# Keys of two chunks placed by tables of slots, a table load of its own, and the positive part moved to VectorE

## The chip, the cores and the metric

The kernel runs on one core of one Trainium2 chip. The metric is the device time in microseconds (us), from the start to the end of one execution. In the rows, PE is TensorE (PEld its weight loads), DVE is VectorE, ACT is ScalarE, POOL is GpSimd and SP is the queue that issues most transfers.

## What is computed

Two layers over 2 x 2048 tokens of width 128, in fp32. Layer 0 is a long convolution through Fourier transforms and a mixture of 8 experts computed densely, with a shared one. Layer 1 is linear attention and a mixture of 8 experts of which each token takes two. The change touches the keys of layer 1's attention and what stands beside them:

```python
def _fm(t):
    return jax.nn.elu(t) + 1.0
q = _fm((x @ wq + bq).reshape(B, N, H, Dh))
k = _fm((x @ wk + bk).reshape(B, N, H, Dh))
v = (x @ wv + bv).reshape(B, N, H, Dh)
kv = jnp.einsum('bnhd,bnhe->bhde', k, v)
z = 1.0 / (jnp.einsum('bnhd,bhd->bnh', q, k.sum(axis=1)) + 1e-06)
scores = jnp.einsum('bnhd,bhde,bnh->bnhe', q, kv, z)
...
topk_scores, topk_idx = jax.lax.top_k(scores, K)
g = jnp.einsum('ner,efr->nef', gate_hidden, W_B)
up = jnp.einsum('nh,efh->nef', x, W_up)
y = jnp.einsum('nef,ehf->neh', jax.nn.silu(g) * up, W_down)
```

Here elu(t) + 1 is computed as max(t, 0) + exp(-max(-t, 0)).

## The kernel before

The tokens are 32 tiles of 128, and 4 tiles are a chunk; there are 8 chunks, numbered 0 to 7. Each engine runs one list of instructions in order, and waits on semaphores. The second half of the program is written as slots: on every engine a loop runs over 90 slots, and in each slot it emits a few steps in a fixed order. Slots 0 to 47 hold layer 0's experts, six slots to a chunk. In each, TensorE multiplies a gate and an up projection (`gate0`, `up0_step`) and, one slot later, the down projection (`down0_step`); ScalarE takes silu of the gate (line 1159) and VectorE multiplies (`product0`, line 1597). `gate0` of a slot stands first on TensorE, then the keys, then `up0_step`. `up0_step` waits until the product of the slot before has read its bank.

Slots 52 to 87 hold layer 1's 36 pairs of blocks of sorted rows: rows are transposed and split in a high and a low part (`turn_rows`, `rows_hi` line 1086, `rows_lo` line 1610), multiplied (`gate_up`), go through silu (line 1093) and a product (`product`, line 1618), which frees the bank that the next pair's `gate_up` needs, and then through the down projection (`turn_products`, `down_rows`). Slots 48 to 51 hold neither: they are the tail of layer 0's last chunks and the head of layer 1.

The work of layer 1's norm, router and attention for chunk c is spread over the slots behind it. `due(s, at)` gives the chunk whose step stands in slot s = 6 (c + 1) + at:

```python
def due(s, at):
    c, rest = divmod(s - at, N0)
    return c - 1 if rest == 0 and 0 <= c - 1 < NCH else None
```

For the keys of chunk c, which are two halves j = 2c and 2c + 1 of two tiles, the steps were: `keys_values` on TensorE, a tile at each of 7, 8, 10, 11; `key_bias` on VectorE at 9 and 12 (line 1580, out of one PSUM bank); `key_features` on ScalarE at 13, for both halves (lines 1076, 1078, 1079: the negative part, the positive part, the exponential) and `query_exp` (line 1133); `key_sum` and `query_features` on VectorE at 14 (lines 1668, 1675); `key_value_sum` on TensorE at 15 and 16. The third tile's `keys_values` waits for the first half's `key_bias`, since both halves use one bank:

```python
if h == 0 and j:
    pe.wait_ge(kv_bias, j)
```

Other steps that are named below: `residual` and its statistics on VectorE at 1 (line 1411), `negated_mean` at 3 (line 1419), `normalise1` on ScalarE at 3 (line 1058), `normed_lo` at 6 (line 1588), the router's gates on TensorE at 7 to 10, their squares on ScalarE at 8 to 11 (line 1067) and sums on VectorE at 9 to 12 (`norm_sum`, line 1462); `rank` (lines 1220 to 1228, 1474) and `tables` (lines 1524 to 1570) on VectorE for every second chunk. silu and exp stand in different tables of ScalarE's functions, and the compiler puts an ACT_TABLE_LOAD where the next function needs the other one.

## Time and profile before

| | us |
|---|---|
| median of 3 runs | 627.75 (625.75 to 628.34) |
| the profiled execution | 624.3 |
| its span | 622.3 |
| busy: PE / DVE / ACT / POOL | 559.3 / 433.8 / 314.8 / 297.3 |

The span is the time from the first to the last instruction of the core; 2.0 us lie around it. The busy times of the engines overlap. Slot 19, where chunk 0's keys are turned to features, starts at 320 us of the span; layer 0's last product is at 430.8 and pair 0's silu at 444.9. Rows of a timeline give the start, the duration, and in brackets the idle time of the engine before the row with what ended it. Consecutive instructions of an engine overlap a little, so the distance from one start to the next is the cost in the stream.

### The profile page before, as it was taken

Reading aid. Unit: us, or ns where it says so; the run is one execution under the profiler, and the core shown is the slowest. Engines: PE = TensorE matmul, PEld = TensorE weight load, DVE = VectorE, ACT = ScalarE, POOL = GpSimd, SP = SyncE. Lnnn points to the kernel's source line nnn. Section 1 sums busy time; section 2 is a strip of 40 time slices with the busy share of each in tenths; the row PEclk is TensorE's granted clock in tenths of the full one; section 3 lists DMA queues with packets and bytes.
Section 4 is the critical chain, followed back from the end, with each engine's and each line's share of the span. In section 5 each row is a group of like instructions: output and inputs, shape, how many; then the busy total and the mean of one; then the engine's idle time right before and its main releaser. Section 6 shows DMA issues by size and latency. Waiting matters only on the chain.

```text
span 622.3 us, 10595 instructions
## 1 busy us (share of the span) xinstructions
PE 559.3 (90%) x3218; PEld 467.3 (75%) x3218; DVE 433.8 (70%) x1151; ACT 314.8 (51%) x623; POOL 297.3 (48%) x268
## 2 busy tenths in 40 slices
PE   5899999999989898999999999998789887899970
PEld 2879986586778676788888888877568777788870
DVE  5958998908941596434565898998878894466673
ACT  4470336764523444144465774675675843365550
POOL 4630030004561355147333446877636775477770
PEclk9999999999999999999999999999999898899995
DMA  7341030410030520323222223303212232233626
GB/s 212 144 203 70 2 135 9 93 43 1 1 136 0 182 111 1 93 71 94 86 81 79 63 73 98 92 27 117 67 53 67 69 107 74 65 86 88 226 85 228
DMA packets 48381, 54.94 MB, mean 88 GB/s; under 512 B 7029, under 2 KB 40374, under 8 KB 47271
## 3 DMA queue, kind: packets, MB, share of 16 engines
q1 hardware_dynamic: 43542, 42.99, 22.1%
q0 software_dynamic: 4320, 8.99, 4.2%
q10 hardware_dynamic: 466, 2.31, 1.7%
q8 instruction: 28, 0.46, 0.3%
q14 instruction: 25, 0.20, 0.1%
HBM read 36.22 MB, written 15.94 MB: 84 GB/s over the span
## 4 chain that ended last, share of the span: by engine, by line
PE 31%; DVE 10%; issue 8%; POOL 7%; ACT 6%; DMA 3%; SPq 0%; POOLq 0%; ACTq 0%; DVEq 0%
PE banks L1759 4%; PE banks L1761 4%; PE banks L1760 4%; PE banks L2116 3%; PE banks L1965 3%; PE banks L1879 2%; DMA arena<-result_rows 2%; POOL arena L887 2%; PE banks L1871 2%; PE banks L2101 2%; POOL result_rows L872 1%; DMA result_rows<-arena 1%; POOL expert_rows L857 1%; PE banks L1892 1%; PE banks L1893 1%
## 5 line engine op out<-in xcount | busy, mean ns | idle before, releaser
L872 POOL DMA_INDIRECT result_rows<-arena x71 | 69.0, 972 | 31.8 <-issue 17.2
L821 POOL TENSOR_TENSOR arena<-arena 128x512 f32<-128x512 f32 x32 | 40.7, 1273 | 86.2 <-DVE arena L1443 86.2
L857 POOL DMA_INDIRECT expert_rows<-arena x64 | 63.2, 988 | 30.9 <-issue 15.8
L887 POOL TENSOR_TENSOR arena<-arena 128x512 f32<-128x512 f32 x32 | 42.4, 1324 | 64.9 <-DVE arena L1597 64.8
L1597 DVE TENSOR_TENSOR arena<-banks,arena 128x512 f32<-128x512 f32 x48 | 33.0, 688 | 42.4 <-PE banks L1761 33.4
L1965 PEld LDWEIGHTS banks<-arena 128*128 128x128 f32 x384 | 48.8, 191 | 7.5 <-POOL arena L887 3.6
L1965 PE MATMUL banks<-arena 128*128 128x128 f32 x384 | 51.6, 277 | 2.5 <-POOL arena L887 1.5
L1871 PE MATMUL banks<-arena 128*128 128x512 f32 x96 | 50.5, 608 | 2.4 <-DVE arena L1443 1.1
L1879 PEld LDWEIGHTS banks<-arena 128*128 128x128 f32 x256 | 33.0, 191 | 19.0 <-POOL arena L821 14.4
L1159 ACT ACTIVATE arena<-banks 128x512 f32<-128x512 f32 x48 | 28.7, 599 | 36.2 <-PE banks L1761 31.7
L2116 PE MATMUL banks<-arena 128*128 x284 | 40.6, 289 | 6.3 <-ACT arena L1110 5.9
L979 ACT ACTIVATE arena<-banks 128x512 f32<-128x512 f32 x48 | 28.7, 597 | 32.5 <-PE banks L1847 32.5
L2116 PEld LDWEIGHTS banks<-arena 128*128 128x128 f32 x284 | 36.8, 202 | 7.4 <-issue 7.4
L1008 ACT ACTIVATE arena<-banks 128x512 f32<-128x512 f32 x32 | 19.1, 597 | 39.5 <-PE banks L1879 39.5
L1441 DVE TENSOR_TENSOR arena<-banks,arena 128x512 f32<-128x512 f32 x32 | 22.1, 692 | 23.7 <-PE banks L1871 22.1
L1879 PE MATMUL banks<-arena 128*128 128x128 f32 x256 | 34.4, 277 | 4.0 <-POOL arena L821 4.0
L1759 PE MATMUL banks<-projection_hi,xnt_hi 128*128 128x384 f32 (+1 forms) x92 | 33.0, 359 | 2.6 <-DVE xnt_lo L1259 2.6
L1759 PE MATMUL banks<-gate_up_weights_hi,rows_hi 128*128 x71 | 32.0, 450 | 3.5 <-DVE arena L1618 3.5
L1450 DVE TENSOR_TENSOR arena<-banks,arena 128x512 f32<-128x512 f32 x16 | 11.1, 692 | 34.5 <-PE banks L1893 34.5
L1618 DVE TENSOR_TENSOR arena<-banks,arena 128x512 f32<-128x512 f32 (+1 forms) x36 | 24.5, 680 | 15.0 <-ACT arena L1093 14.7
L1093 ACT ACTIVATE arena<-banks 128x512 f32<-128x512 f32 (+1 forms) x36 | 21.4, 594 | 24.0 <-PE banks L1761 23.9
L1110 ACT ACTIVATE arena<-banks,arena 128x128 f32<-128x128 f32 x71 | 22.2, 364 | 21.7 <-DMA result_rows<-arena 11.5
(277 smaller groups left out, 1625.7 us busy)
## 6 DMA issues: line engine op xcount, KB each, us to landing
arena<-expert_weights SPq DMA_DIRECT2D x64, 128.0 KB, 3.4
arena<-expert_rows SPq DMA_DIRECT2D x71, 66.0 KB, 1.9
arena<-in_x SPq DMA_DIRECT2D x8, 512.0 KB, 7.0
arena<-result_rows SPq DMA_DIRECT2D x8, 512.0 KB, 5.7
arena<-in_dft_f SPq DMA_DIRECT2D x1, 2048.0 KB, 9.5
normed_hi<-xnt_hi SPq DMA_DIRECT2D x1, 2048.0 KB, 6.7
normed_lo<-xnt_lo SPq DMA_DIRECT2D x1, 2048.0 KB, 11.1
arena<-in_dft_i SPq DMA_DIRECT2D x1, 2048.0 KB, 7.6
```

The source lines that it names most:

```text
L821: nc.gpsimd.tensor_tensor(out=T1[:, q % 3, :], in0=T1[:, q % 3, :], in1=T2[:, q % 2, :], op=ALU.add).then_inc(y_in, 1)
L857: pool.indirect_dma_start(out=xrows, out_offset=bass.IndirectOffsetOnAxis(ap=SLOT[:, k, t:t + 1], axis=0), in_=XNF[:, t, :], in_offset=Non ...
L872: pool.indirect_dma_start(out=yrows, out_offset=bass.IndirectOffsetOnAxis(ap=DEST[:, i, n:n + 1], axis=0), in_=YB[:, i % YBUFS, n, :], in_ ...
L887: nc.gpsimd.tensor_tensor(out=AM0[slot % 2], in0=AM0[slot % 2], in1=WB0[:, m, :], op=ALU.mult).then_inc(weighted, 1)
L979: nc.scalar.activation(spread_rows(n % NI), bank(spread_bank(n % NI), 2, NGR, 4), ACT.Copy)\
L1159: nc.scalar.activation(SG0, PS[0], ACT.Silu).then_inc(silu_done, 1)
L1597: nc.vector.tensor_tensor(out=AM0[n % 2], in0=PS[1], in1=SG0, op=ALU.mult).then_inc(mult_done, 1)
L1759: mm(o, lh, rh, start=start, stop=False, skip_group_check=True)
L1871: mm(PS[2 + J % 2], TURNF, ZT[:, J % 2, :], start=True, stop=True).then_inc(d_mm, 1)
L1879: ins = mm(PS[6 + q % 2][:, P * n:P * (n + 1)], T1[:, q % 3, P * n:P * (n + 1)], TURNI, start=True, stop=True)
L1965: ins = mm(PS[2][:, D * t:D * (t + 1)], AM0[n % 2][:, P * t:P * (t + 1)], DW0[:, m, :], start=False, stop=(m == N0 - 1), skip_group_check= ...
L2116: ins = mm(PS[6][:, P * s:P * (s + 1)], AMT[:, i % 2, 2 * s + f, :], DN_FLAT[:, at], start=(f == 0), stop=(f == 1), skip_group_check=True)
```

## The change

Tables of slots, one entry for each chunk, take the place of the fixed numbers. Chunks 0 to 4 keep theirs. Chunk 5's third and fourth tile come one slot earlier, and so does everything behind them (features in slot 48, sums in 49, `key_value_sum` in 50). Chunk 6's keys come in slots 49 and 50, its biases in 50 and 51, its features in 51 (they were in 55), its sums in 52, its products in 53 and 54. Chunk 7's first negative part comes at 10 and not at 13. On ScalarE the negative parts of both halves now stand ahead of both exponentials; the positive part (line 1078) is gone, and VectorE's sum takes it in one scalar_tensor_tensor. Behind chunk 6's exponentials a silu of one column is added, whose result nobody reads.

```diff
+KEYS_AT = (*((7, 8, 10, 11),) * 5, (7, 8, 9, 10), (7, 7, 8, 8), (7, 8, 10, 11))
+KEY_BIAS_AT = (*((9, 12),) * 5, (9, 11), (8, 9), (9, 12))
+KEY_NEG_AT = (*((13, 13),) * 5, (12, 12), (9, 9), (10, 13))
+KEY_EXP_AT = (*(13,) * 5, 12, 9, 13)
+KEY_SUMMED_AT = (*(14,) * 5, 13, 10, 14)
+KEY_VALUE_AT = (*((15, 16),) * 5, (14, 14), (11, 12), (15, 16))
...
+        def chunks_due(s, table):
+
+            return [c for c in range(NCH) if s == N0 * (c + 1) + table[c]]
+
+        def parts_due(s, table):
+
+            return [(c, n) for c in range(NCH) for n, at in enumerate(table[c]) if s == N0 * (c + 1) + at]
...
-            def key_features(j):
+            def key_negative(j):
...
                 nc.scalar.activation(KEX[:, j % 3], k, ACT.Relu, scale=-1.0).then_inc(k_neg, 1)
+            def key_exp(j):
+
                 act.wait_ge(k_neg, j + 1)
-                nc.scalar.activation(k, k, ACT.Relu)
                 nc.scalar.activation(KEX[:, j % 3], KEX[:, j % 3], ACT.Exp, scale=-1.0).then_inc(k_exp, 1)
...
-                c = due(slot, 13)
-                if c is not None:
-                    key_features(2 * c)
-                    key_features(2 * c + 1)
+                for c, h in parts_due(slot, KEY_NEG_AT):
+                    key_negative(2 * c + h)
+                for c in chunks_due(slot, KEY_EXP_AT):
+                    key_exp(2 * c)
+                    key_exp(2 * c + 1)
                     query_exp(c)
+                    if c == NCH - 2:
+                        act.wait_ge(k_sum, 2 * c)
+                        nc.scalar.activation(KEX[:, (2 * c - 1) % 3, 0, 0:1], BQ, ACT.Silu)
...
-                nc.vector.tensor_tensor(out=k, in0=k, in1=KEX[:, j % 3], op=ALU.add).then_inc(k_sum, 1)
+                nc.vector.scalar_tensor_tensor(out=k, in0=k, scalar=0.0, in1=KEX[:, j % 3], op0=ALU.max,
+                                               op1=ALU.add).then_inc(k_sum, 1)
...
+                for c, t in parts_due(slot, KEYS_AT):
+                    keys_values(TPC * c + t)
```

The changed file's lines are 14 to 20 further down. What the tables do to the lists of instructions, at three places:

TensorE in slot 45, before. The first three rows are `gate0`, the next three `up0_step`, L2052 is `key_value_sum`.

```order
L1759 MATMUL banks<-normed_chunk_hi,gate_weights_hi 128x512 [waits silu_done]
L1760 MATMUL banks<-normed_chunk_lo,gate_weights_hi 128x512
L1761 MATMUL banks<-normed_chunk_hi,gate_weights_lo 128x512
L1759 MATMUL banks<-normed_chunk_hi,up_weights_hi 128x512 [waits mult_done]
L1760 MATMUL banks<-normed_chunk_lo,up_weights_hi 128x512
L1761 MATMUL banks<-normed_chunk_hi,up_weights_lo 128x512
L2052 MATMUL banks<-arena 128x129 [waits kv_mask,k_sum]
```

The same place of the changed kernel:

```order
L1777 MATMUL banks<-normed_chunk_hi,gate_weights_hi 128x512 [waits silu_done]
L1778 MATMUL banks<-normed_chunk_lo,gate_weights_hi 128x512
L1779 MATMUL banks<-normed_chunk_hi,gate_weights_lo 128x512
L1777 MATMUL banks<-qkv_weights_hi,normed_hi 128x256 [waits kv_bias]
L1778 MATMUL banks<-qkv_weights_lo,normed_hi 128x256
L1779 MATMUL banks<-qkv_weights_hi,normed_lo 128x256
L1777 MATMUL banks<-normed_chunk_hi,up_weights_hi 128x512 [waits mult_done]
```

The keys of chunk 5's third tile, with their wait for the first half's bias, now stand ahead of slot 45's up projection.

VectorE in slots 49 to 51, before, from the end of `residual`: L1220 to L1228 are `rank` of the third router batch, L1668 and L1675 the sums of chunk 5, L1580 the first `key_bias` of chunk 6.

```order
L1206 TENSOR_SCALAR arena<-arena 128x4 [waits dve_chain]
L1220 TENSOR_TENSOR arena<-arena 128x512 [waits log1_in]
L1221 TENSOR_TENSOR arena<-arena 128x512 [waits dve_chain]
L1668 TENSOR_TENSOR arena<-arena 128x2x128 [waits k_exp,dve_chain]
L1668 TENSOR_TENSOR arena<-arena 128x2x128 [waits k_exp]
L1675 TENSOR_TENSOR arena<-arena 128x512 [waits q_pos,q_exp]
L1227 TENSOR_TENSOR arena<-arena 128x512
L1228 TENSOR_TENSOR arena<-arena 128x512 [waits dve_chain]
L1610 TENSOR_TENSOR rows_lo<-banks,rows_hi 128x256 [waits xt_hi,dve_chain]
L1580 TENSOR_TENSOR arena<-banks,arena 128x2x256 [waits kvs_mm,kv_mm]
L1419 SCALAR_TENSOR_TENSOR arena<-arena 128x4 [waits ln1_rstd]
```

And changed:

```order
L1226 TENSOR_SCALAR arena<-arena 128x4 [waits dve_chain]
L1688 SCALAR_TENSOR_TENSOR arena<-arena 128x2x128 [waits k_exp] x2
L1696 TENSOR_TENSOR arena<-arena 128x512 [waits q_pos,q_exp]
L1240 TENSOR_TENSOR arena<-arena 128x512 [waits log1_in]
L1241 TENSOR_TENSOR arena<-arena 128x512 [waits dve_chain]
L1600 TENSOR_TENSOR arena<-banks,arena 128x2x256 [waits kvs_mm,kv_mm,dve_chain]
L1247 TENSOR_TENSOR arena<-arena 128x512
L1248 TENSOR_TENSOR arena<-arena 128x512 [waits dve_chain]
L1630 TENSOR_TENSOR rows_lo<-banks,rows_hi 128x256 [waits xt_hi,dve_chain]
L1600 TENSOR_TENSOR arena<-banks,arena 128x2x256 [waits kvs_mm,kv_mm]
L1439 SCALAR_TENSOR_TENSOR arena<-arena 128x4 [waits ln1_rstd]
```

Chunk 6's first bias stands between the two halves of `rank`, and its second ahead of `negated_mean`; chunk 5's second bias, further up, is gone from slot 48.

ScalarE in slots 51 and 52, before: `rows_hi`, a square, `normalise1` of chunk 7 in two rows, `rows_hi` of pair 1, a square, and pair 0's silu with its table load.

```order
L1086 ACTIVATE rows_hi<-banks 128x256 [waits xt_mm]
L1067 ACTIVATE arena<-banks 128x512 [waits log1_in,gh_mm]
L1058 ACTIVATE arena<-arena 128x128 [waits ln1_nmr]
L1058 ACTIVATE arena<-arena 128x128 x3
L1086 ACTIVATE rows_hi<-banks 128x256 [waits xt_mm]
L1067 ACTIVATE arena<-banks 128x512 [waits log1_in,gh_mm]
L1093 ACT_TABLE_LOAD
L1093 ACTIVATE arena<-banks 128x512 [waits gu_mm]
```

And changed:

```order
L1072 ACTIVATE arena<-arena 128x128 [waits ln1_nmr]
L1072 ACTIVATE arena<-arena 128x128 x3
L1090 ACTIVATE arena<-arena 128x256 [waits kvs_mm,kv_bias] x2
L1095 ACTIVATE arena<-arena 128x256 [waits k_neg] x2
L1149 ACTIVATE arena<-arena 128x512 [waits q_neg]
L1196 ACT_TABLE_LOAD
L1196 ACTIVATE arena<-arena 128x1 [waits k_sum]
L1102 ACTIVATE rows_hi<-banks 128x256 [waits xt_mm]
L1081 ACTIVATE arena<-banks 128x512 [waits log1_in,gh_mm]
L1109 ACTIVATE arena<-banks 128x512 [waits gu_mm]
```

Five activations, the load and the one-column silu now stand ahead of pair 1's `rows_hi`. Slots 55 and 56 have lost an exp load and a silu load: the changed program has 18 table loads in all, and the one before 20.

## Rows read from the trace of the kernel before

**Rows 1.** The page: busy time and share of each engine.

```profile
PE 559.3 (90%) x3218; PEld 467.3 (75%) x3218; DVE 433.8 (70%) x1151; ACT 314.8 (51%) x623; POOL 297.3 (48%) x268
```

**Rows 2.** Windows: length, busy PE, PEld, DVE, ACT, POOL, granted clock, DMA share, GB/s.

```profile
320.40:409.30 88.90, 88.26 (x551) 76.75 (x550) 75.33 (x191) 58.05 (x110) 51.85 (x42) 1.00 0.26 76
```

**Rows 3.** Timeline of ScalarE in slot 19: chunk 0's features.

```profile
320.94 0.41 ACT L1076 ACTIVATE arena<-arena 128x256 f32<-128x256 f32 x1
321.38 0.42 ACT L1078 ACTIVATE arena<-arena 128x256 f32<-128x256 f32 x1
...
324.49 0.62 ACT L1133 ACTIVATE arena<-arena 128x512 f32<-128x512 f32 x1
```

**Rows 4.** Timeline of VectorE, slots 45 to 47: chunk 5's first bias, then products.

```profile
422.65 0.69 DVE L1580 TENSOR_TENSOR arena<-banks,arena 128x512 f32<-128x512 f32 x1
...
423.32 0.69 DVE L1597 TENSOR_TENSOR arena<-banks,arena 128x512 f32<-128x512 f32 x1
...
430.77 0.69 DVE L1597 TENSOR_TENSOR arena<-banks,arena 128x512 f32<-128x512 f32 x1 [1.70 <-ACT arena L1159]
```

**Rows 5.** Timeline of TensorE: slot 45's up projection, and slot 46's keys.

```profile
419.61 0.50 PE L1759 MATMUL banks<-normed_chunk_hi,up_weights_hi 128*128 128x512 f32 x1 [0.58 <-DVE arena L1597]
...
423.39 0.39 PE L1759 MATMUL banks<-qkv_weights_hi,normed_hi 128*128 128x256 f32 x1
```

**Rows 6.** Timeline of VectorE, slots 49 to 51.

```profile
433.76 0.68 DVE L1411 TENSOR_TENSOR arena<-banks,arena 128x512 f32<-128x512 f32 x1
...
435.88 0.68 DVE L1220 TENSOR_TENSOR arena<-arena 128x512 f32<-128x512 f32 x1
...
437.33 0.77 DVE L1668 TENSOR_TENSOR arena<-arena 128x256 f32<-128x256 f32 x2
...
438.62 0.68 DVE L1227 TENSOR_TENSOR arena<-arena 128x512 f32<-128x512 f32 x1
...
440.06 0.42 DVE L1610 TENSOR_TENSOR rows_lo<-banks,rows_hi 128x256 fp32r<-128x256 f32 x1
440.40 0.68 DVE L1580 TENSOR_TENSOR arena<-banks,arena 128x512 f32<-128x512 f32 x1
```

**Rows 7.** Timeline of ScalarE, slots 51 and 52: the stretch ahead of pair 0's silu.

```profile
441.19 1.65 ACT L1058 ACTIVATE arena<-arena 128x128 f32<-128x128 f32 x4 [3.07 <-DVE arena L1419]
...
443.60 1.28 ACT L1093 ACT_TABLE_LOAD   x1
444.90 0.60 ACT L1093 ACTIVATE arena<-banks 128x512 f32<-128x512 f32 x1
```

**Rows 8.** Timeline of VectorE, slots 55 to 57: the end of `tables`, pairs 4 and 5.

```profile
459.42 0.81 DVE L1538 TENSOR_TENSOR arena<-arena 128x16 f32<-128x16 f32 x4
461.58 0.42 DVE L1610 TENSOR_TENSOR rows_lo<-banks,rows_hi 128x256 fp32r<-128x256 f32 x1 [1.36 <-ACT rows_hi L1086]
463.90 0.69 DVE L1618 TENSOR_TENSOR arena<-banks,arena 128x512 f32<-128x512 f32 x1 [1.90 <-ACT arena L1093]
```

**Rows 9.** Timeline of TensorE: four rows that follow an idle stretch.

```profile
440.63 0.41 PE L2072 MATMUL banks<-arena 128*128 128x128 f32 x2 [1.40 <-DVE rows_lo L1610]
...
489.62 1.09 PE L2101 MATMUL banks<-arena 128*128 128x128 f32 x4 [2.15 <-ACT arena L1100]
...
524.21 0.79 PE L2116 MATMUL banks<-arena 128*128 x2 [2.88 <-ACT arena L1110]
...
536.96 0.75 PE L2116 MATMUL banks<-arena 128*128 x3 [2.12 <-ACT arena L1110]
```

**Rows 10.** Windows behind the first two of these stretches, columns as in rows 2.

```profile
441.00:443.00 2.00, 1.92 (x9) 1.31 (x9) 1.93 (x8) 1.81 (x5) 1.52 (x2) 1.00 0.22 72
490.00:491.00 1.00, 1.00 (x7) 1.00 (x6) 0.55 (x2) 0.98 (x2) 0.79 (x1) 0.50 0.26 68
```

**Rows 11.** Groups by form on VectorE: count, busy us, mean ns, idle before.

```profile
L1668 DVE TENSOR_TENSOR arena<-arena 128x256 f32<-128x256 f32 x16 | 6.8, 463 | 0.8 <-ACT arena L1079 0.6
L1371 DVE SCALAR_TENSOR_TENSOR arena<-arena 64x1024 f32<-64x1024 f32 x2 | 2.4, 1207 | 0.0
```

More of the change, by code:

```diff
@@ L1690, in _ @@
                     residual(c)
-                for h in range(2):
-                    c = due(slot, 9 + 3 * h)
-                    if c is not None:
-                        key_bias(2 * c + h)
+                for c, h in parts_due(slot, KEY_BIAS_AT):
+                    key_bias(2 * c + h)
                 c = due(slot, 17)
@@ L1709, in _ @@
                     places_of(i)
-                c = due(slot, 14)
-                if c is not None:
+                for c in chunks_due(slot, KEY_SUMMED_AT):
                     key_sum(2 * c)
@@ L2176, in _ @@
                     turn_normed(c)
-                for h in range(2):
-                    c = due(slot, 15 + h)
-                    if c is not None:
-                        key_value_sum(2 * c + h)
+                for c, h in parts_due(slot, KEY_VALUE_AT):
+                    key_value_sum(2 * c + h)
                 c = query_due(slot, 0)
```

4 lines of the change are left out of this document (removed).

## The prediction

> **What bounds the kernel now.** I read the page first. TensorE is busy for 559.3 of 622.3 us, VectorE 434, ScalarE 315 [rows 1]. That is an average, so I took windows by stage. In layer 0's experts, 320.4 to 409.3 us, TensorE is busy 88.26 of 88.90 us [rows 2]: nothing that another engine saves there can show. The timelines then gave what each moved step does in its place: ScalarE's features [rows 3], the end of layer 0 on VectorE and TensorE [rows 4, 5], the head of layer 1 on VectorE and ScalarE [rows 6, 7], and the pairs behind it, where the three engines wait for each other in turn [rows 8]. From about 420 us on a delay on any of the three tends to reach the end, because a pair's product frees the bank of the next.
>
> **The positive part.** ScalarE loses two operations a chunk. One lies between 321.38 and the load, and the two together take 0.87 us: from 320.94 to 324.49 the features need 3.55 us, and 2.68 without them [rows 3]. For chunks 0 to 4 this is hidden under the full TensorE; I take -0.3 us, with 0 and 5 x 0.87 = -4.3 as bounds. VectorE's sum becomes a scalar_tensor_tensor. No such operation of 128x256 is in the trace. The additions take 463 ns in the mean, and a scalar_tensor_tensor of 1024 columns takes 1207 [rows 11]: (1207 - 463) / 768 = 0.97 ns a column, no more than an addition pays (0.69 us for 512, [rows 4]; 0.42 for 256, [rows 6]: 1.05 ns). So 0. Upper bound 0.25 us each, one more pass of 256 columns at that rate; 16 of them make 4 us. It may also be below the 463, which holds waiting for a shared port at most; that would give 16 x 0.04 = 0.6.
>
> The Trainium skill ("Vector Engine (DVE) Microarchitecture Reference", section 7, "Points that are easy to get wrong") says that a scalar_tensor_tensor with two sources in SBUF that aren't both bf16 runs at half the rate. By it each sum would take near 0.69 us, which is the upper bound just given. The 1207 ns of the 1024-column row don't agree with it; whether its operands are of that kind in every respect, no row shows.
>
> **Chunk 5's third tile (stall A).** It waits for chunk 5's first bias, and now stands ahead of slot 45's up projection. That bias runs at 422.65 on VectorE, behind `tables`, and is over at about 423.35 [rows 4]. TensorE has finished the gate at 419.0, and before the change started the up projection at 419.61, after 0.58 idle [rows 5]. Now it stands still until 423.35: 4.3 us of idle. The keys take 0.45, the up projection starts at 423.8 (+4.2). Its product ran at 423.32 [rows 4], since VectorE was held by `tables`: now 424.7 (+1.4). On TensorE the work of 419.61 to 423.39 stands behind; 0.36 comes back because slot 46's keys are gone from there, 0.6 of waits, and the product of slot 47 had 1.70 idle in front of it [rows 4]. It moves from 430.77 to 432.8 (+2.0). `residual` of chunk 7 moves by less, as chunk 5's second bias (0.69) is gone from before it: 433.76 [rows 6] to 435.2 (+1.4).
>
> **Chunk 6's keys (stall B).** Its third and fourth tile now stand in slot 50 and wait for its first bias. On VectorE that bias stands behind `residual` with its statistics (433.76 to 435.88, 2.1 us), the sums of chunk 5 (437.33 to 438.62, 1.3) and the first half of `rank` (435.88 to 437.33, 1.4) [rows 6]: 435.2 + 2.1 + 1.3 + 1.4 = 440.0, done at 440.7. In that time TensorE has done its router product and the two first tiles and waits for about 4 us. Then come the two key tiles (0.8), chunk 5's `key_value_sum` (0.9), the router's gates (0.8), `turn_rows` (0.4), and on ScalarE `rows_hi` (0.4): the first `rows_lo` goes from 440.06 [rows 6] to 444.1, **+4.0**. `negated_mean` stands behind it and behind the second bias, and `normalise1` goes from 441.19 [rows 7] to 445.2.
>
> **Features and table load.** Ahead of pair 0's silu on ScalarE there now stand two negative parts, two exponentials and the query's: 0.45 + 0.4 + 0.3 + 0.3 + 0.5, 1.8 us less a little by the distances of [rows 3], plus 0.3 for the silu of one column and its wait. The load of 1.28 only moves: it stood just before that silu, at 443.60 [rows 7]. Pair 0's silu was bound by ScalarE's own list, `normalise1` included, so the whole 2.1 is paid: 444.90 to 451.0, **+6.1** in all. On VectorE chunk 6's sums and query features, 1.3 us, stand in slot 52 ahead of the router's `norm_sum`, whose result the next square on ScalarE waits for, and behind that square stands pair 1's silu: **+1.2**. Together +7.3.
>
> **What comes back.** In slots 55 and 56 chunk 6's features with both their loads are gone. VectorE stood idle 1.36 and 1.90 us there: it had finished `tables` at 459.42 + 0.81 = 460.23, and `product` ran only at 463.90 [rows 8]. With only `rows_lo` (0.34 in the stream) between, -3.3. The sums and query features behind it, -1.3. Chunk 6's second bias out of slot 54, -0.2. At chunk 7 the same exponentials and loads stay, but one negative and both positive parts are gone in front of ScalarE's copy for which TensorE waits 2.15 us at 489.62 [rows 9]: -1.2. With -0.3 from layer 0 this makes -6.3, and +7.3 - 6.3 = **+1.0 us** at full clock.
>
> **The clock.** TensorE stands idle before four rows of [rows 9]. After 1.40 us at 440.63 the granted clock stays 1.00, 2.4 GHz; after 2.15 at 489.62 it is 0.50, 1.2 GHz [rows 10]. The same was so after 2.88 and 2.12 us at 524.21 and 536.96 [rows 9]. The price is seen at 489.62: four transposes take 1.09 us where the same count at full clock takes 0.60 or so, and the work up to the next full-clock row some 3.4 us in place of 1.8, **1.6 us**. Stalls A and B are both over 4 us, in places where TensorE does everything that follows: 2 x 1.6 = +3.2. No row has a fall directly behind layer 0's dense stage, so 0 to 3.3 each are the bounds (the longest low stretch, after 524.21, is twice as long). Sum: +1.0 + 3.2 = **+4.2 us**, 624.3 to 628.5 for the profiled execution; the median shown is 3.45 above it, so 627.75 + 4.2 = **632.0**.
>
> **Rivals.** A change by less than about 0.5% (3.1 us) can't be told from none in a measurement of this kernel.
> - *Stalls and clock falls*, the forecast: +4.2, own range +2.5 to +7 (630.2 to 634.7). Chance 0.46. For it: the order of the rows and the wait leave TensorE no choice in slot 45.
> - *Stalls at full clock, or partly taken up*: A's +1.4 at `residual` vanishes if VectorE has slack there, and no clock is lost: +1.0 down to -0.4, so 627 to 630. Chance 0.27. Against it: three falls in three idle stretches over 2 us. For it: the stalls are behind long dense work, and those three are not.
> - *Faster*, the other side: the wait in slot 50 doesn't bind, because VectorE comes to chunk 6's first bias before TensorE needs its bank. It is then free of the +4.0, and pays only 2.1 + 1.2 against 6.3: -3.0, and with part of the 4.3 hidden in layer 0 coming through, -3 to -5: 623 to 625. It decides at about 436 us for that bias; my sum has 440.0, and would have to count `rank` and the sums (2.7) and A (1.4) wrongly. Chance 0.20.
> - *The sum at half rate*: 16 x 0.25 = 4 us on VectorE, of which some 3 in places where it is waited for (the last chunks and their neighbours): 635. Chance 0.05; this is the rule named above.
> - *The silu of one column saves nothing because the load stays where it was*: the compiler's list already shows it at the new place, so this rival has 0.02, at +4.2 as well.
>
> **How the numbers follow.** The likeliest case gives 632.0. Slower by over 0.5% (above 630.9): most of the first case, 0.40, nearly all of the rate case and the last, 0.07: 0.47. Faster (below 624.6): 0.18 of the third and 0.04 of gains in layer 0 beside the second: 0.22. The rest, 0.31, lies between. The range of 623.5 to 634.5 leaves out the far end of the faster case, the half-rate case and a long low clock.
>
> **What the changed profile would show.** A: TensorE idle for about 4.3 us before keys (line 1777), released by VectorE's line 1600, and the up projection behind it near 423.8. B: a second such idle, some 4 us, before keys 3 and 4 of chunk 6, and the first `rows_lo` (line 1630) near 444. Granted clock 0.50 behind each. Line 1688 at about 0.42 to 0.46 us; 0.69 would be the half rate. One ACT_TABLE_LOAD with line 1196, none in slots 55 and 56, and pairs there at the 4 us of their neighbours. Chunk 7: a shorter idle before line 2119. I am wrong if the first stall is short, if the clock stays at 1.00 behind them, or if pair 0's silu isn't near 451.

## The result, and the profile after

The changed kernel takes 634.62 us in the median of 4 runs (630.37 to 637.33), and the kernel before 626.75 in the median of 4 (623.67 to 628.34). The ratio is 1.0159 with a 95% interval of 1.0111 to 1.0208: slower, +7.9 us by the medians. Forecast was +4.2 us, with a range up to 634.5. The direction, and the two stalls that were to make it, are right; the size is not. Below, "stall A" and "stall B" are the two of the prediction, a "fall" is a stretch in which TensorE's granted clock is 0.50 (1.2 GHz) and not 1.00 (2.4 GHz), and "low" means time in such stretches.

The page of the changed kernel, busy time and share (before: [rows 1]). ScalarE lost 8 us, TensorE's busy time grew by 10 with the same number of instructions:

```profile
PE 569.2 (90%) x3218; PEld 477.0 (75%) x3218; DVE 434.2 (68%) x1151; ACT 306.8 (48%) x606; POOL 297.6 (47%) x268
```

TensorE, timeline of slot 45 and of slots 50 to 53 (before: [rows 5, 9]):

```profile
424.92 0.40 PE L1779 MATMUL banks<-normed_chunk_hi,gate_weights_lo 128*128 128x512 f32 x1
429.66 0.38 PE L1777 MATMUL banks<-qkv_weights_hi,normed_hi 128*128 128x256 f32 x1 [4.34 <-DVE arena L1600]
...
448.45 0.58 PE L1777 MATMUL banks<-qkv_weights_hi,normed_hi 128*128 128x256 f32 x1 [3.67 <-DVE arena L1600]
...
449.89 1.92 PE L2070 MATMUL banks<-arena 128*128 128x129 f32 x8
...
454.48 0.79 PE L1777 MATMUL banks<-router_weights_hi,normed_hi 128*128 128x512 f32 x1 [0.96 <-ACT arena L1081]
...
460.91 0.59 PE L1777 MATMUL banks<-router_weights_hi,normed_hi 128*128 128x512 f32 x1 [1.92 <-ACT arena L1081]
```

Stall A is 4.34 us (forecast 4.3) and stall B 3.67 (forecast about 4), both before keys and both ended by the bias, line 1600. A third wait, 1.92 us before a router product at 460.91, wasn't forecast as one of TensorE.

VectorE in slots 45 and 49 to 51 (before: [rows 4, 6]):

```profile
428.92 0.69 DVE L1600 TENSOR_TENSOR arena<-banks,arena 128x512 f32<-128x512 f32 x1
...
442.87 0.68 DVE L1431 TENSOR_TENSOR arena<-banks,arena 128x512 f32<-128x512 f32 x1
...
444.98 0.76 DVE L1688 SCALAR_TENSOR_TENSOR arena<-arena 128x256 f32<-128x256 f32 x2
445.65 0.68 DVE L1696 TENSOR_TENSOR arena<-arena 128x512 f32<-128x512 f32 x1
446.25 0.69 DVE L1240 TENSOR_TENSOR arena<-arena 128x512 f32<-128x512 f32 x1
446.97 0.69 DVE L1241 TENSOR_TENSOR arena<-arena 128x512 f32<-128x512 f32 x1
447.70 0.69 DVE L1600 TENSOR_TENSOR arena<-banks,arena 128x512 f32<-128x512 f32 x1
...
454.05 0.42 DVE L1630 TENSOR_TENSOR rows_lo<-banks,rows_hi 128x256 fp32r<-128x256 f32 x1 [4.33 <-ACT rows_hi L1102]
```

Between `residual` and the bias that TensorE waits for stand the sums and half of `rank`, 444.98 to 447.70. Then VectorE itself waits 4.33 us for `rows_hi`, which waits for TensorE's late work.

ScalarE in slots 51 and 52 (before: [rows 7]):

```profile
455.17 1.65 ACT L1072 ACTIVATE arena<-arena 128x128 f32<-128x128 f32 x4 [0.74 <-DVE arena L1439]
456.73 0.71 ACT L1090 ACTIVATE arena<-arena 128x256 f32<-128x256 f32 x2
457.35 0.71 ACT L1095 ACTIVATE arena<-arena 128x256 f32<-128x256 f32 x2
457.96 0.62 ACT L1149 ACTIVATE arena<-arena 128x512 f32<-128x512 f32 x1
458.60 1.28 ACT L1196 ACT_TABLE_LOAD   x1
459.89 0.20 ACT L1196 ACTIVATE arena<-arena 128x1 f32<-128x1 f32 x1
460.00 0.37 ACT L1102 ACTIVATE rows_hi<-banks 128x256 fp32r<-128x256 f32 x1
460.26 0.59 ACT L1081 ACTIVATE arena<-banks 128x512 f32<-128x512 f32 x1
460.74 0.60 ACT L1109 ACTIVATE arena<-banks 128x512 f32<-128x512 f32 x1
```

The list runs without a gap from `normalise1` to pair 0's silu; the square at 460.26 is what TensorE's router product at 460.91 waited for.

Windows, columns as in [rows 2]: layer 0's experts, two windows behind stalls A and B, and the stage from 410 to 470 us:

```profile
327.20:415.60 88.40, 87.93 (x551) 76.66 (x550) 75.31 (x191) 55.17 (x102) 51.79 (x42) 1.00 0.27 76
431.50:433.50 2.00, 2.00 (x12) 2.00 (x11) 2.00 (x3) 0.00 (x0) 1.26 (x1) 0.50 0.00 0
449.00:456.00 7.00, 6.04 (x23) 4.84 (x22) 2.65 (x6) 1.70 (x5) 2.08 (x2) 0.50 0.08 20
410.00:470.00 60.00, 46.43 (x236) 38.10 (x234) 45.12 (x129) 30.46 (x62) 35.81 (x33) 0.86 0.18 56
```

The granted clock of 0.50 lasts from 447.5 to 457.8 us, 10 us: it begins inside stall B, which ends at 448.45. In [rows 10] it was about 3.4 us long behind one idle stretch.

The same window of the kernel before:

```profile
410.00:470.00 60.00, 49.30 (x284) 38.46 (x282) 50.00 (x163) 40.88 (x83) 38.59 (x37) 1.00 0.24 71
```

A mean clock of 0.86 over 60 us, with two levels of 1 and 0.5, is 0.14 x 2 x 60, about 17 us at 1.2 GHz; before it is none. The prediction had reckoned with two stretches of 3.4 us.

**Where the time went.** I lined the traces up by the starts of the same instruction. Chunk 0's `residual`, ahead of which nothing is changed, starts at 282.71 before and 289.49 after: 6.8 us late. That is no part of the change. In that execution the clock had fallen in the convolution, behind idle times of 0.88, 0.97 and 0.69 us that the kernel before has as well without a fall (0.89, 0.96, 0.69). So I count from chunk 0's `residual`. The second trace of the changed kernel (below) has no such fall. Lateness against before, in us:

| at | forecast at full clock (with its falls) | first trace | second trace |
|---|---|---|---|
| residual of chunk 6 (end of dense stage) | -0.3 | -0.5 | -0.5 |
| residual of chunk 7 | +1.1 (+2.7) | +2.3 | +2.0 |
| first `rows_lo` | +3.7 (+6.9) | +7.2 | +5.6 |
| pair 0's silu | +5.8 (+9.0) | +9.1 | +7.5 |
| pair 1's product | +7.0 (+10.2) | +11.4 | +9.9 |
| pair 3's product | +7.0 (+10.2) | +11.3 | +10.9 |
| pair 5's product | +2.2 (+5.4) | +6.4 | +6.4 |
| pair 10's product | +1.0 (+4.2) | +5.1 | +5.0 |
| pair 17's product | +1.0 (+4.2) | +6.1 | +5.9 |
| end | +1.0 (+4.2) | +6.1 | +3.4 |

### The profile page after: what moved, and what is told of

Same layout as the page of the kernel before. It is cut to its first block, busy times and chain, and to the rows that moved or that the text cites. A ratio compares the mean times of both kernels' runs of the same rounds, so it can differ in the third digit from the quotient of the medians.

```text
span 635.2 us, 10577 instructions
## 1 busy us (share of the span) xinstructions
PE 569.2 (90%) x3218; PEld 477.0 (75%) x3218; DVE 434.2 (68%) x1151; ACT 306.8 (48%) x606; POOL 297.6 (47%) x268
## 3 DMA queue, kind: packets, MB, share of 16 engines
q10 hardware_dynamic: 466, 2.31, 1.7%
## 4 chain that ended last, share of the span: by engine, by line
PE 37%; DVE 9%; POOL 7%; issue 6%; ACT 3%; DMA 3%; SPq 0%; POOLq 0%; ACTq 0%; DVEq 0%
PE banks L1777 5%; PE banks L1779 5%; PE banks L1778 5%; PE banks L1983 4%; PE banks L2134 3%; POOL expert_rows L871 3%; PE banks L1897 2%; DMA arena<-result_rows 2%; PE banks L1889 2%; POOL result_rows L886 1%; PE banks L2119 1%; PE banks L1910 1%; DMA result_rows<-arena 1%; PE banks L1911 1%; PE banks L2070 1%
## 5 line engine op out<-in xcount | busy, mean ns | idle before, releaser
L1983 PEld LDWEIGHTS banks<-arena 128*128 128x128 f32 x384 | 49.6, 194 | 6.1 <-POOL arena L901 3.1
L1983 PE MATMUL banks<-arena 128*128 128x128 f32 x384 | 52.3, 280 | 1.4 <-POOL arena L901 1.3
L1897 PEld LDWEIGHTS banks<-arena 128*128 128x128 f32 x256 | 34.5, 199 | 19.0 <-POOL arena L835 14.4
L1175 ACT ACTIVATE arena<-banks 128x512 f32<-128x512 f32 x48 | 28.8, 600 | 36.4 <-PE banks L1779 31.7
L993 ACT ACTIVATE arena<-banks 128x512 f32<-128x512 f32 x48 | 28.7, 597 | 34.5 <-PE banks L1865 34.5
L2134 PEld LDWEIGHTS banks<-arena 128*128 128x128 f32 x284 | 36.1, 199 | 8.2 <-issue 8.2
L1897 PE MATMUL banks<-arena 128*128 128x128 f32 x256 | 36.1, 286 | 4.0 <-POOL arena L835 4.0
L1022 ACT ACTIVATE arena<-banks 128x512 f32<-128x512 f32 x32 | 19.1, 597 | 41.2 <-PE banks L1897 41.2
L1630 DVE TENSOR_TENSOR rows_lo<-banks,rows_hi 128x256 fp32r<-128x256 f32 (+1 forms) x36 | 15.1, 418 | 31.6 <-ACT rows_hi L1102 31.4
L1081 ACT ACTIVATE arena<-banks 128x512 f32<-128x512 f32 x32 | 19.1, 598 | 34.0 <-PE banks L1779 24.4
```

The costliest lines, as they stand in the source:

```text
L1897: ins = mm(PS[6 + q % 2][:, P * n:P * (n + 1)], T1[:, q % 3, P * n:P * (n + 1)], TURNI, start=True, stop=True)
L1983: ins = mm(PS[2][:, D * t:D * (t + 1)], AM0[n % 2][:, P * t:P * (t + 1)], DW0[:, m, :], start=False, stop=(m == N0 - 1), skip_group_check= ...
L2134: ins = mm(PS[6][:, P * s:P * (s + 1)], AMT[:, i % 2, 2 * s + f, :], DN_FLAT[:, at], start=(f == 0), stop=(f == 1), skip_group_check=True)
```

## The experiments

In all runs, times are medians, with the ratio to the kernel before on the same chip and its 95% interval. "Counted" means late against before from chunk 0's `residual`, as in the table.

**1. The sum alone.** The kernel before with one edit.

```diff
-                nc.scalar.activation(k, k, ACT.Relu)
...
-                nc.vector.tensor_tensor(out=k, in0=k, in1=KEX[:, j % 3], op=ALU.add).then_inc(k_sum, 1)
+                nc.vector.scalar_tensor_tensor(out=k, in0=k, scalar=0.0, in1=KEX[:, j % 3], op0=ALU.max,
+                                               op1=ALU.add).then_inc(k_sum, 1)
```

> The kernel before with one edit: the positive part goes from ScalarE into VectorE's sum, nothing moves. Theory (rate of an addition): line 1667's scalar_tensor_tensor of 128x256 takes 0.42 to 0.46 us, layer 0 gains about 0.5 us (the changed kernel's residual of chunk 7 came 0.5 us less late than that of chunk 0), slots 55 and 61 gain 0.87 us each where silu waits for ScalarE: -1.5 to -2.3 us in all. Rival (half rate): 0.69 us a sum, and up to +3 us. Rival (nothing shows): 0.

622.8 us, ratio 0.9975 (0.9938 to 1.0013). Its trace, groups by form on VectorE, and the same group of the changed kernel (before: [rows 11]):

```profile
L1667 DVE SCALAR_TENSOR_TENSOR arena<-arena 128x256 f32<-128x256 f32 x16 | 7.2, 489 | 0.3 <-ACT arena L1078 0.2
```

```profile
L1688 DVE SCALAR_TENSOR_TENSOR arena<-arena 128x256 f32<-128x256 f32 x16 | 6.9, 470 | 0.6 <-ACT arena L1095 0.5
```

463 ns for the addition, 489 and 470 for the operation in its place. The fused operation costs no more than 0.03 us, and the rival of half the rate is out. The Trainium skill ("Vector Engine (DVE) Microarchitecture Reference", section 7) has fp32 sources in SBUF at half the rate; this case measures 470 to 489 ns for 256 columns and doesn't agree. Counted, -0.5 comes from layer 0, -0.7 from slot 55, -0.7 from chunk 7, and the end is -2.2. By the medians the run can't be told from no change.

**2 and 3. One chunk back.** The tables' entries of chunk 5 as before (run 2), or of chunk 6, without the one-column silu (run 3).

```diff
-KEYS_AT = (*((7, 8, 10, 11),) * 5, (7, 8, 9, 10), (7, 7, 8, 8), (7, 8, 10, 11))
+KEYS_AT = (*((7, 8, 10, 11),) * 6, (7, 7, 8, 8), (7, 8, 10, 11))
```

```diff
-KEYS_AT = (*((7, 8, 10, 11),) * 5, (7, 8, 9, 10), (7, 7, 8, 8), (7, 8, 10, 11))
+KEYS_AT = (*((7, 8, 10, 11),) * 5, (7, 8, 9, 10), (7, 8, 10, 11), (7, 8, 10, 11))
```

(and the five other tables in the same way.)

> The changed kernel with chunk 5's entries of all tables as before; chunk 6 and 7 as changed. Theory (each stall has its own price): the 4.34 us of idle in slot 45 are gone with the low clock behind them, residual of chunk 7 comes 2.8 us earlier than in the changed kernel against the same residual of chunk 0, and the whole takes about 2.8 us less than the changed kernel: some 3.4 us above before by the profile. The second stall stays near 3.7 us, since VectorE's list ahead of chunk 6's first bias is what makes it. Rival (the two stalls are in series): stall B grows by what A gives back and the time stays that of the changed kernel. Rival (clock falls elsewhere make the difference): no change in the stage, and the time moves only by what other falls do.

625.45 us, 1.0034 (0.9994 to 1.0074). Counted, residual of chunk 7 -0.5, first `rows_lo` +0.1, end -1.8. That is 7.9 us less than the changed kernel's first trace and 5.2 less than its second, where I had expected 2.8. Stall B had shrunk to 2.40, and the clock stayed up behind it:

```profile
437.71 0.39 PE L1777 MATMUL banks<-qkv_weights_hi,normed_hi 128*128 128x256 f32 x1 [2.40 <-DVE arena L1600]
...
447.14 0.80 PE L1777 MATMUL banks<-router_weights_hi,normed_hi 128*128 128x512 f32 x1 [2.91 <-ACT arena L1081]
```

The fall in this trace, 446.5 to 453.3, goes with the router product's wait of 2.91 us. With chunk 5's sums back in slot 50, they stand on VectorE behind chunk 6's first bias and not ahead of it: my expectation overlooked that the edit moves them too. So chunk 5's earlier slots charge twice, at stall A and by their sums ahead of B. My sentence that VectorE's list stays was wrong.

> The changed kernel with chunk 6's entries of all tables as before and no silu of one column; chunk 5's stay one slot earlier, chunk 7's negative part early, the sum as changed. Theory: stall A stays (+2.8 at residual of chunk 7), layer 0 -0.5, the second bias of chunk 5 out of slot 48 is in that already, no stall B and no features in front of pair 0, chunk 6's features in slot 55 shorter by 0.87, chunk 7's by 1.2: +2.8 - 0.9 - 1.2 = about +0.7 us against before. Rival (stall B is a consequence of A): a second idle over 3 us in slots 49 to 51 shows here too, and the time is 4 us or more above before.

625.35 us, 1.002 (0.9986 to 1.0053). Counted, residual of chunk 7 +3.0, unchanged up to pair 3, +2.1 behind slots 55 and 56, +0.9 behind chunk 7, end +0.2. Stall A is there alone (4.32 us), with no second idle over 1.4 us behind it before pair 16. A doesn't make B. The fall with it is 6.8 us long here (420.5 to 427.3), where the changed kernel's two traces have 3.5 and 3.4 with the same stall:

```profile
420.00:428.00 8.00, 5.74 (x22) 5.27 (x23) 5.35 (x14) 1.65 (x4) 4.25 (x4) 0.57 0.06 18
```

**4. Chunk 5 back, and chunk 6's first bias a slot earlier.**

```diff
-KEY_BIAS_AT = (*((9, 12),) * 5, (9, 11), (8, 9), (9, 12))
+KEY_BIAS_AT = (*((9, 12),) * 6, (7, 9), (9, 12))
```

> As the run with chunk 5 as before, and chunk 6's first bias one slot earlier on VectorE (7 in place of 8: right behind residual, ahead of the sums of chunk 5 and the first half of rank). Theory: neither stall over 1.5 us, no clock fall between 410 and 460 us, first rows_lo less than 1 us later than before against chunk 0's residual. What is left: +2.1 for the features in front of pair 0's silu, +1.2 for the sums in slot 52, -5.0 from slots 55 and 56, -1.2 from chunk 7, -0.5 from layer 0: about -3.4 us against before. Rival (the stalls aren't the price, ScalarE's and VectorE's added work is): first product of the pairs still more than 6 us late, total above before. Rival (the bank, not the order on VectorE): keys of the third tile still wait over 3 us.

623.3 us, 0.9985 (0.9945 to 1.0024). The idle before the third tile is 0.96 us, first `rows_lo` 0.0, pair 0's silu +2.0 (forecast for that term: +2.1). But pair 1's product is at +4.2 and pair 3's at +5.2, not +3.3. The end is -0.8, not -3.4: with both stalls gone, the third wait has become the longest, with falls at 452.4 and 459.3, and 0.9 is lost again between pairs 16 and 17.

```profile
451.96 0.50 PE L1777 MATMUL banks<-router_weights_hi,normed_hi 128*128 128x512 f32 x1 [2.92 <-ACT arena L1081]
452.30 0.51 PE L1778 MATMUL banks<-router_weights_lo,normed_hi 128*128 128x512 f32 x1
452.60 0.63 PE L1779 MATMUL banks<-router_weights_hi,normed_lo 128*128 128x512 f32 x1
```

Router products of 0.39 us at full clock take 0.63 here.

**5 and 6. One entry each.** Chunk 6's first bias at 7 in place of 8 (stall A stays), and chunk 5's first bias at 8 in place of 9 (stall B stays), in the changed kernel.

```diff
-KEY_BIAS_AT = (*((9, 12),) * 5, (9, 11), (8, 9), (9, 12))
+KEY_BIAS_AT = (*((9, 12),) * 5, (9, 11), (7, 9), (9, 12))
```

```diff
-KEY_BIAS_AT = (*((9, 12),) * 5, (9, 11), (8, 9), (9, 12))
+KEY_BIAS_AT = (*((9, 12),) * 5, (8, 11), (8, 9), (9, 12))
```

> The changed kernel with one entry altered: chunk 6's first bias at 7 in place of 8, so that it stands on VectorE behind residual and ahead of chunk 5's sums and of rank. Stall A stays. Against before, counted from chunk 0's residual, the changed kernel had +2.3 us at chunk 7's residual, +7.2 at the first rows_lo, +6.1 at the end; the run with chunk 5 as before had -0.5, +0.1, -1.8. Theory (chunk 5's sums and rank in front of the bias make stall B, its idle of 3.67 us and the 9 us of low clock behind it): residual of chunk 7 stays +2.3, first rows_lo +3, no fall at 448 us, end +2 to +3. Rival (stall A's delay reaches stall B and makes it, whatever the order on VectorE): first rows_lo still +6 or more, end +5 or more.

> The changed kernel with one entry altered: chunk 5's first bias at 8 in place of 9, one slot earlier on VectorE, so that its third tile finds the bank free. Stall B's order stays (chunk 5's sums and rank ahead of the bias). Theory (two prices that add): the 4.34 us idle in slot 45 and the fall behind it are gone, chunk 7's residual -0.5 to -1.0 us (also the second bias of chunk 5 is out of slot 48), stall B still over 3 us with a fall of the clock, first rows_lo +3.5 to +4.5, end +2.5 to +3.5. Rival (A makes B): no idle over 2 us in slot 50, first rows_lo under +1, end -1.5 to -2, as in the run with chunk 5 as before.

Run 5: 632.26 us, 1.0108 (1.0059 to 1.0157); counted +2.0 at chunk 7's residual, +2.6 at the first `rows_lo`, +6.8 at pair 1, +0.6 at pair 10, end -0.5. Run 6: 628.54 us, 1.0069 (1.0036 to 1.0101); -1.1, +3.0, +7.3, +1.0, end +1.4. The first three numbers are near what the theory of two prices has (run 6's +3.0 was +3.5 at the least): A alone +2.6 at the first `rows_lo`, B alone +3.0, neither 0.0 (run 4), both +5.6 and +7.2. The ends miss, by 2.5 and 1.1 us low: run 5 gets 1.9 us back between pairs 17 and 23, where its trace has one fall and not two, and run 6 was 0.5 low from the first `rows_lo` on. The medians of both lie more above before than their traces' ends (6.6 and 2.9 us in place of -0.5 and +1.4); one trace is one draw. By the medians run 5 gives back little: 1.0108 against 1.0159 and 1.0127 of the changed kernel, with two of its six executions near 625 us and four at 631.7 to 633.5. That stall B has a price of its own rests on the milestones of the traces. Run 6's rows show when the clock falls:

```profile
438.72 0.38 PE L1777 MATMUL banks<-qkv_weights_hi,normed_hi 128*128 128x256 f32 x1 [3.72 <-DVE arena L1600]
...
439.53 1.74 PE L2070 MATMUL banks<-arena 128*128 128x129 f32 x8
...
441.92 0.63 PE L1779 MATMUL banks<-router_weights_hi,normed_lo 128*128 128x512 f32 x1
...
444.27 0.40 PE L1778 MATMUL banks<-router_weights_lo,normed_hi 128*128 128x512 f32 x1
```

Behind stall B alone the keys still run at full clock, the rows slow down from 439.5 on, and full clock is back by 444.

**7. TensorE kept at work in stall B.**

```diff
+                if slot == 50:
+                    pe.wait_ge(mult_done, N0 * NCH)
+                    for n in range(12):
+                        mm(PS[1], XNH[:, 0:P], WAH[:, :, :], start=True, stop=True)
```

> The changed kernel with twelve matmuls of 128x512 ahead of chunk 6's keys in slot 50, into a bank that nobody reads; TensorE works through most of stall B, which itself stays. Theory (half of stall B's price is the clock): the clock stays 1.00 through 447 to 457 us, the first rows_lo is 0.5 to 1 us and the second product 2 to 3 us earlier than in the changed kernel (+7.2 and +11.4), the end +3.5 to +4. Rival (only the wait counts, the low clock lies under other engines' work): no difference beyond 0.5 us at the second product. Rival (the clock doesn't follow idle time but its own course): low again in the same stretch.

The window that answers to the changed kernel's 449 to 456:

```profile
449.00:456.00 7.00, 5.29 (x32) 4.01 (x30) 4.56 (x15) 3.99 (x11) 3.88 (x4) 1.00 0.15 42
```

Clock 1.00 where it was 0.50; first `rows_lo` +5.0, pair 1's product +9.2, end +3.5. Both milestones are 2.2 us earlier than in the first trace of the changed kernel, whose low stretch was 10 us long, and 0.6 to 0.7 earlier than in the second (run 8), where it was 7: the price of this one fall lies on both sides of the 1.6 that I had counted. The keys themselves aren't delayed: they start at 448.43 here and at 448.45 in the changed kernel, both behind the bias at 447.7. The whole takes 634.27 us in the median, 1.0144 (1.0102 to 1.0186), no less than the changed kernel: the third wait is 3.37 us here, and a fall of 6.8 us goes with it. The stage has some 10 us low in place of 17.

**8. The changed kernel again.** Unaltered.

> The changed kernel once more, unaltered, for its size in many executions and a second trace. Its first trace showed the end +6.1 us counted from chunk 0's residual, and +6.8 us ahead of that residual, where the two kernels are the same; there the granted clock had fallen in the convolution (170 to 190 and 250 to 260 us) behind idles of 0.88 and 0.97 us. Theory (the change itself costs 6 us, the rest is how often the clock falls in the convolution): the second trace shows again 4.3 us idle in slot 45, about 3.7 in slot 50, first rows_lo +7 and end +6 from chunk 0's residual, whatever stands before it; median 6 to 8 us above before. Rival (the low clock of 9 us behind stall B was chance): first rows_lo +5, end +4.

631.76 us, 1.0127 (1.0089 to 1.0165). Stalls of 4.35 and 3.67 us; counted +5.6 at the first `rows_lo`, +5.0 at pair 10, end +3.4; chunk 0's `residual` 0.5 late. Its stage:

```profile
410.00:470.00 60.00, 46.72 (x242) 38.45 (x241) 44.87 (x138) 31.21 (x65) 31.78 (x30) 0.86 0.19 58
```

Again about 17 us at 1.2 GHz, with a low stretch of 6.8 us at B, 443.3 to 450.1. With both stalls this stretch is 10 and 7 us long in two traces, and with B alone it was 3.4 (run 6). But the rival, that its length was chance, fits as well or better: it had +5 at the first `rows_lo` and +4 at the end, the theory +7 and +6, and the trace has +5.6 and +3.4. Nor is a long fall bound to an earlier stall: stall A's was 6.8 us in run 3 with nothing ahead of it, and the third wait's was 6.8 in run 2, without A, and 3.4 in runs 5, 6 and in this one.

**9. The kernel before against itself.** No edit.

> The kernel before against itself: what the comparison gives where there is no difference, and a second trace of it. Theory (falls of the clock in the convolution come by chance, some in each kernel): ratio 1.000 within 0.4%; if its trace has a fall there, chunk 0's residual is 4 to 7 us late and everything behind it stands as in the first trace. Rival (only the changed kernels fall there): none of its executions is at 628 us or more.

623.03 us, 0.9984 (0.9947 to 1.002). Every milestone of the table is within 0.1 us of the first trace, and the end within 0.2. Its executions run from 620.42 to 628.74 us: the scatter is of the program, not of the change. One thing differs from the first trace, and it bears on the price of a fall. The stretch of [rows 9] at 489.62, with 2.15 us of idle and a fall, stands here at 489.30, with the same idle and no fall: four transposes in 0.63 us, not 1.09.

```profile
489.30 0.63 PE L2101 MATMUL banks<-arena 128*128 128x128 f32 x4 [2.15 <-ACT arena L1100]
...
492.73 0.49 PE L1759 MATMUL banks<-gate_up_weights_hi,rows_hi 128*128 x1 [1.03 <-DVE arena L1618]
```

Yet pair 10's product and all behind it up to pair 17 come within 0.04 us of the first trace. At full clock TensorE is done sooner and then waits 1.03 us for VectorE's product, so that this row stands 3.4 us behind the transposes with the fall (493.07) and without it. From this very stretch the prediction had taken its 1.6 us for a fall; at the end of the program this fall cost nothing.

**10. What loses nothing.** Chunks 5 and 6 as before, the sum as changed, chunk 7's first negative part at 10.

```diff
+KEY_NEG_AT = (*((13, 13),) * 7, (10, 13))
```

> The kernel before with the two parts of the change that lost nothing: the positive part in VectorE's sum, and chunk 7's first negative part at 10. Chunks 5 and 6 as before. The sum alone gave -2.2 us from chunk 0's residual. Theory: chunk 7 gives 0.45 more at pairs 9 and 10 (-1.2 in all there), of which a part is lost again at pair 17, whose result copy waits for stored rows: end -2.2 to -2.7, 0.3 to 0.4% less. Rival (the early negative part delays pair 7's product by its own 0.45): -2.2 or less gain.

623.93 us, 0.9972 (0.9938 to 1.0007). Counted -2.5 at pair 10 (the sum alone: -2.0), -1.6 at pair 17, end -3.3 where -2.2 to -2.7 was expected; behind pair 17 its clock falls at other places than before's. Its chunk 0 `residual` is 6.7 us late, with clocks of 0.89, 0.77, 0.97 and 0.68 in the convolution: windows of 10 us from 170 to 190 and 240 to 260. A kernel whose chunks 5 and 6 are as before falls there too.

**11 and 12. All causes mended.** Chunk 5's first bias at 8, chunk 6's biases at 7 and 8, its features in slot 50 and its sums at 9; the one-column silu behind chunk 7's `normalise1`.

```diff
-KEY_BIAS_AT = (*((9, 12),) * 5, (9, 11), (8, 9), (9, 12))
-KEY_NEG_AT = (*((13, 13),) * 5, (12, 12), (9, 9), (10, 13))
-KEY_EXP_AT = (*(13,) * 5, 12, 9, 13)
-KEY_SUMMED_AT = (*(14,) * 5, 13, 10, 14)
+KEY_BIAS_AT = (*((9, 12),) * 5, (8, 11), (7, 8), (9, 12))
+KEY_NEG_AT = (*((13, 13),) * 5, (12, 12), (8, 8), (10, 13))
+KEY_EXP_AT = (*(13,) * 5, 12, 8, 13)
+KEY_SUMMED_AT = (*(14,) * 5, 13, 9, 14)
...
                    normalise1(c)
+                    if c == NCH - 1:
+                        act.wait_ge(k_sum, 2 * c - 2)
+                        nc.scalar.activation(KEX[:, (2 * c - 3) % 3, 0, 0:1], BQ, ACT.Silu)
```

> Both biases as in the two runs above (chunk 5's first at 8, chunk 6's at 7 and 8), chunk 6's negative parts and exponentials at 8, in slot 50, ahead of rows_hi of pair 0 and of normalise1, its sums at 9, and the one-column silu behind chunk 7's normalise1 in slot 51. Theory (what is left of the loss is ScalarE's list between normalise1 and pair 0's silu, 2.1 us, and the square behind it with TensorE's 2.9 us idle before a router product): no idle of TensorE over 2 us between 415 and 500 us, pair 0's silu under +0.7 us, second product under +1, and all of -5.0 of slots 55 and 56 and -1.2 of chunk 7 kept: end -5 to -6 us against before, time 0.8 to 1.0% less. Rival (features ahead of rows_hi of pair 0 delay the whole head): first rows_lo +1.5 or more and the end -3 or less gain.

623.38 us, 0.9957 (0.9931 to 0.9983). Counted: first `rows_lo` +0.7, pair 0's silu +0.3, pair 1 +0.3, pair 5 -4.7, end -5.3. The time is 0.4% less, where 0.8 to 1.0% was expected. An idle of 2.86 us, with a fall, was left before a router product, where none over 2 was expected: the second negative part waits 2.14 us for its bias, and the square stands behind it. In run 12 the features stand in slot 51, between the square and `normalise1`:

```diff
                if c is not None:
+                    if c == NCH - 1:
+                        for j in (2 * c - 2, 2 * c - 1):
+                            key_negative(j)
+                        for j in (2 * c - 2, 2 * c - 1):
+                            key_exp(j)
+                        query_exp(c - 1)
                    normalise1(c)
```

> The last combination with chunk 6's negative parts and exponentials in slot 51, behind rows_hi of pair 0 and the square, ahead of normalise1; before it they were in slot 50, where the second waited 2.1 us for its bias with rows_hi and the square behind it, and TensorE stood idle 2.86 us before a router product. Theory: rows_hi of pair 0 and the square run early, no idle of TensorE over 2 us in 415 to 500, clock 1.00 there, pair 0's silu within 0.3 us of before, pair 4's product -4 and the end -5.5 to -6.5 from chunk 0's residual. Rival (VectorE's rank and biases set normalise1 anyhow): end the same -5.3.

622.08 us, 0.9964 (0.9937 to 0.999). Pair 0's silu is at -0.3, pair 4's product -4.0, the end -5.9, and no idle over 1.3 us stands between 415 and 500 us:

```profile
410.00:470.00 60.00, 52.71 (x314) 42.32 (x313) 54.23 (x181) 39.28 (x83) 40.94 (x39) 1.00 0.26 75
```

Both versions take 0.4% less than the kernel before, with intervals that end at 0.9983 and 0.999, and so beat the changed kernel too; between them the measurement doesn't tell.

## Why the prediction was wrong

**Right.** The dense stage hid ScalarE's gain (-0.5 for -0.3). Stall A: 4.34 us of idle for 4.3, and chunk 7's residual 2.3 and 2.0 late where the sum had 2.7 with its fall. Stall B: its place and its cause, with `rank` and the sums ahead of the bias (run 5 takes them away, and the idle is 0.95). ScalarE's list: +2.1 forecast, +1.9 between the first `rows_lo` and the silu in both traces. Slots 55 and 56: -4.8 forecast, -4.8 and -4.6 between pairs 3 and 5. Chunk 7: -1.2 forecast, -1.2 at pair 10 in both traces. The fused operation at the addition's rate.

**The step that failed** is "2 x 1.6 = +3.2", the clock. It was right that the clock falls at both stalls, and wrong how long and how often: two stretches of 3.4 us were counted, and the stage from 410 to 470 us had about 17 us low in both traces. Three things were off in it, and a fourth beside it.
- *The price of one fall.* The 1.6 us were read at 489.62, as time that TensorE's own work took. Run 9 shows that this fall cost the program nothing, since the next work of TensorE waited for VectorE anyway. A fall is paid only where TensorE is what the stage waits for; the 1.6 was no measured price, and that the forecast's total came near the traces' ends (+6.1 and +3.4) owes something to luck.
- *The length at B.* I took one stretch of some 3.4 us as the measure of each fall. At B the low clock lasted 10 and 7 us; against the run with the filler that cost 2.2 and 0.6 us.
- *A third fall.* The term "+1.2 for the sums" saw only VectorE. What follows it on TensorE, a router product that waits for the square behind ScalarE's longer list, stood idle for 1.9 us (1.8 in the second trace, and 2.9 to 3.4 in runs 2 and 4 to 7), with a low stretch behind it at 460 to 464. Pair 1's product lost 2.4 us more than pair 0's silu in both traces, not 1.2; by pair 3 the second trace had lost 1.1 more, with a fall at 460.4.
- *The gain that doesn't pass*, which is no part of the clock: a loss that the sum put at nothing. Between pairs 16 and 17 the changed kernel loses 0.9 to 1.0 us again, as do the runs whose chunk 7 is shortened (0.5 in run 1). There ScalarE's result copy waits for the rows of earlier pairs to be stored, 5.3 us before and 6.2 after. TensorE's idle there, 2.88 us in [rows 9], became 3.95. Most of what chunk 7's slots gave ends there.

ScalarE at that place, before and changed:

```profile
523.33 0.62 ACT L1110 ACTIVATE arena<-banks,arena 128x128 f32<-128x128 f32 x2 [5.27 <-DMA result_rows<-arena]
```

```profile
536.18 0.63 ACT L1126 ACTIVATE arena<-banks,arena 128x128 f32<-128x128 f32 x2 [6.19 <-DMA result_rows<-arena]
```

By the milestones the sum is then -0.5 + 11.9 - 5.1 - 1.2 + 1.0 = +6.1 in the first trace. The second has 1.6 less at pair 1, is 0.3 less by pair 3, and loses 2.6 less behind pair 17, where its clock fell for less time than before's.

**What the medians add.** The changed kernel is 7.9 and 6.0 us above before by the medians, its traces' ends 6.1 and 3.4. The executions themselves answer this. The time at 1.2 GHz of an execution is 2 x (1 - mean clock) x span. A line through 96 executions of the kernel before gives 612.2 + 0.42 x that time, and one through the 10 of the changed kernel 614.1 + 0.40 x it. At 40 us low that is 629.0 and 630.1: by this line the change costs **about 1 us** at the same clock, near what the full-clock sum said. The line is good to 2 us at best: it puts run 1, whose trace ends 2.2 us early, at +0.4, and run 7, whose trace ends as late as the changed kernel's second, at +2.8. The means are 30.6 and 46.3 us low, and 15.7 x 0.42 = **6.6 us** is the rest of the 7.4 by which the mean times differ (632.5 and 625.1). The stage from 410 to 470 us alone has about 17 us low in both traces and none before. The milestones give less for the stage: 11.3 and 10.9 at pair 3, against 7.0 at full clock, are about **4 us**. The Trainium skill ("TensorE: Matmul & The Clock Gate", Terms) prices the time at the lower clock at half of it, which would be an estimate of 7.9 us for the 15.7; the executions give 0.42 of it, a little less. Of the low time of every trace 14 to 18 us lie behind TensorE's last matmul and cost nothing (the prediction took the 6.8 us after 524.21 for the longest stretch); they are nearly the same in all and drop out of the difference. Falls in the convolution, ahead of the change, don't drop out: they are in the 6.6. So the clock term should have been about 4 us by the milestones and some 6.6 by the executions, not 3.2. The line is a correlation; that the clock costs time in this stage is shown by the filler, and that a long idle brings falls by run 4, where stall B and the fall behind it are both gone, and by run 12, where the whole stage has neither.

**Open.** Where the clock's share lies, at 4 us, at 6.6 or beside both, since one trace of an execution is one draw. Why a fall lasts 3.4, 6.8 or 10 us with the same idle. And why the filler's median is no lower than the changed kernel's, although its stage is some 7 us less at the low clock: of 6 executions five are at 633.6 or more. Over whole executions the filler saved little low time, 44.4 us in the mean against 46.3, so it took away one fall of a trace and not the low time of the program.

**Base of the sum.** I added +4.2 to a median of three executions, 627.75, and took one trace for the kernel. With a fourth execution that median is 626.75, so 1.0 of the 3.7 us between forecast and measured difference is the base. Executions of before alone range from 620.4 to 632.4 us, and the slower ones have more low time (it goes from 21 to 47 us). In five of fourteen traces chunk 0's `residual` was 4.8 to 6.8 us late, behind falls in the convolution: in four with changed slots for chunks 5 or 6 and in run 10, which has them as before. Neither trace of the kernel before has such a fall, so that it falls there too isn't shown, and whether the changed kernel has these falls more often can't be told from so few.

## What to carry to other kernels

When a step is put earlier in the list of an engine that waits, ask what it waits for and what stands ahead of that on the other engine, also after the other edits of the same change have moved their own work there: chunk 5's sums made stall B 3.67 us long where it was 2.40 without them. Price an idle of TensorE of some 2 us or more twice, once as the wait and once as the slow stretch that may come with it (here 3.4 to 10 us long, or none), but the second only where the stage waits for TensorE; and look for the next wait that shows when this one is mended. Where executions of one program scatter by 10 us, count lateness from the last point ahead of the change, and look at how much of each was at the low clock.
